# Gated delta rule: layout of the keys' norm row in DRAM, and a wait ahead of the next weights' load

## The reference, cut to what matters

```
mixed = silu(conv(x @ W_qkvz))            # causal convolution, four taps
q, k, v = ...                             # q, k: [B, S, 16, 128]
k = k * rsqrt(sum(k * k, axis=-1) + 1e-6) # one factor for each token and key head
# then, in chunks of tokens, with decay and beta:
M = -tril((k_beta @ k.T) * decay, -1);  T = inverse(I - M)
attn = (q @ k.T) * decay;  state update and output from k, q, v, T, attn
x = layernorm(x + gated_output @ W_out);  x = layernorm(x + ffn(x))
```

## Time and profile before

| | us |
|---|---|
| median of three runs | 4628.52 |
| lowest and highest of them | 4620.41, 4631.1 |
| the profiled execution, own time | 4659.61 |
| its span, first to last instruction | 4657.8 |
| PE busy in the span | 4215.2 |
| ACT busy | 3830.0 |
| DVE busy | 3657.7 |
| POOL busy | 2368.6 |
| mean granted TensorE clock | 0.979 of full speed |

### The profile page before, as it was taken

The page is one execution under the profiler, slowest core; times in us unless marked ns, Lnnn a source line. Parts: engine busy times, 40 slices in busy tenths (PEclk is TensorE's granted clock), DMA queues, the critical chain, the costliest instruction groups (busy, mean ns, idle before and its releaser), DMA issues. The chain is left out here.

```text
span 4657.8 us, 139558 instructions
## 1 busy us (share of the span) xinstructions
PE 4215.2 (90%) x44242; PEld 3757.0 (81%) x44242; DVE 3657.7 (79%) x6626; ACT 3830.0 (82%) x10831; POOL 2368.6 (51%) x3362
## 2 busy tenths in 40 slices
PE   3399999999999999999999999999999999999497
PEld 2288888888888888888888888888888888888476
DVE  4288888888888888888888888888888888888454
ACT  1388888888898888988889888898898988888244
POOL 4355555555545555455555555555555555555244
PEclk9699999999999999999999999999999999999799
DMA  6544443433434344343343443433434434343000
GB/s 196 187 138 125 130 140 122 138 125 130 143 122 134 125 129 144 121 134 128 127 144 124 131 133 123 143 123 132 134 123 142 125 130 139 121 140 107 32 14 23
DMA packets 365392, 584.77 MB, mean 126 GB/s; under 512 B 148240, under 2 KB 228624, under 8 KB 347920
## 3 DMA queue, kind: packets, MB, share of 16 engines
q1 hardware_dynamic: 364560, 583.70, 38.9%
q10 hardware_dynamic: 768, 0.26, 0.0%
HBM read 533.81 MB, written 50.07 MB: 125 GB/s over the span
## 5 line engine op out<-in xcount | busy, mean ns | idle before, releaser
L924 DVE SCALAR_TENSOR_TENSOR conv<-ps,cws,conv 128x511 f32<-128x511 f32 (+2 forms) x1536 | 1084.9, 741 | 68.2 <-ACT conv L812 56.8
L1116 POOL TENSOR_TENSOR xo<-xo,zs 128x512 f32<-128x512 f32 x256 | 326.3, 1275 | 1559.5 <-DVE xo L1018 1559.5
L630 PE MATMUL ps<-xb,wb 128*128 128x512 f32 x3072 | 841.1, 409 | 76.9 <-DMA wb<-w_scratch 73.3
L630 PEld LDWEIGHTS ps<-xb,wb 128*128 128x128 f32 x3072 | 541.8, 190 | 169.8 <-issue 73.5
L967 DVE CAST_PREDICATED pl<-masks,ps 128x512 f16<-128x512 uint16 x768 | 544.7, 709 | 56.2 <-PE ps L692 32.5
L873 ACT ACTIVATE t<-ps 128x512 f16<-128x512 f32 x768 | 465.3, 606 | 119.3 <-PE ps L700 108.5
L877 ACT ACTIVATE u<-ps 128x512 f16<-128x512 f32 x768 | 463.5, 604 | 43.7 <-PE ps L705 43.7
L790 PE MATMUL ps<-wo,xt 128*128 128x256 f32 x3072 | 427.9, 289 | 25.3 <-issue 23.4
L644 PE MATMUL ps<-wb,xb 128*128 128x256 f32 x3072 | 430.1, 290 | 0.0
L812 ACT ACTIVATE conv<-ps,cws 128x512 f32<-128x512 f32 x512 | 360.0, 703 | 69.7 <-PE ps L630 61.5
L790 PEld LDWEIGHTS ps<-wo,xt 128*128 128x128 f32 x3072 | 382.5, 189 | 39.4 <-issue 34.5
(11 more groups left out here) (158 smaller groups left out, 11557.9 us busy)
## 6 DMA issues: line engine op xcount, KB each, us to landing
xb<-x_scratch SPq DMA_DIRECT2D x128, 1024.0 KB, 5.9
wb<-w_scratch SPq DMA_DIRECT2D x128, 1024.0 KB, 7.5
grow<-rows_scratch SPq DMA_DIRECT2D x128, 512.0 KB, 3.7
wb<-w_scratch SPq DMA_DIRECT2D x128, 512.0 KB, 4.2
wo<-wout_scratch SPq DMA_DIRECT2D x128, 512.0 KB, 6.2
rk<-rk_scratch SPq DMA_DIRECT2D x128, 256.0 KB, 5.5
w_scratch<-wsplit SPq DMA_DIRECT2D x128, 192.0 KB, 3.4
wpiece<-in_Wqkvz SPq DMA_DIRECT2D x128, 96.0 KB, 2.1
```

The lines of the kernel that those rows point to most:

```text
L630: last = nc.tensor.matmul(proj_bank[c][:, :], wb[:, pw, k * WCOL + c * D:k * WCOL + (c + 1) * D], xb[p][:, px, k * S:(k + 1) * S], start=( ...
L924: nc.vector.scalar_tensor_tensor(out=conv[c][:, back:S], in0=proj_bank[c][:, 0:S - back], scalar=cws[p][:, c * TAPS + 3 - back:c * TAPS + ...
L1116: nc.gpsimd.tensor_tensor(x, x, zs[p][:, 2 * g:2 * g + 2, :, :], ALU.mult).then_inc(gated.sem, 1)
```

## The change

Three edits, in three places of `delta_rule`:

1. `load_w` of item a now also waits until the load of `rk` of item a - 1 has landed. That is the load that SP issued directly before it.
2. `store_norm` writes `rn` transposed: token i of chunk n goes to place n x 128 + i of the row in DRAM, where before it went to place i x 4 + n. The four numbers of a partition, which were one run of 16 bytes, are four runs of 4 bytes.
3. `keys` reads `rk` in steps of one element, where before it read every fourth element.

```
             def load_w(a, p, _):
                 proj_mm.wait(sp, a - 1, 4)
+                rk_in.wait(sp, a - 1, 16)
                 sp.dma_start(w_dst[:, :, 0:S], ...).then_inc(w_in.sem, 16)
...
             def store_norm(a, p, _):
                 sp.wait_ge(rnorm.sem, rnorm.at(a, 1))
                 rk_in.wait(sp, a - 1, 16)
-                sp.dma_start(rk_dram[0].rearrange("(i n) -> i n", n=NC), rn[:, :]).then_inc(rk_out.sem, 16)
+                sp.dma_start(rk_dram[0].rearrange("(n i) -> i n", n=NC), rn[:, :], allow_slow_non_contiguous=True).then_inc(rk_out.sem, 16)
...
                 nc.vector.tensor_tensor(kq[p][:, :, 0, :], conv[K][:, :].rearrange("p (n c) -> p n c", n=NC),
-                                        rk[:, :].rearrange("p (c n) -> p n c", n=NC), ALU.mult).then_inc(kq_ready.sem, 1)
+                                        rk[:, :].rearrange("p (n c) -> p n c", n=NC), ALU.mult).then_inc(kq_ready.sem, 1)
```

## The result

The changed kernel takes 5699.21 us (median of four runs, 5693.95 to 5701.22) against 4629.81 us before in the same session. The ratio is 1.2312, with a 95% interval of 1.2293 to 1.233: 23% slower, over a thousand microseconds, or 8.4 us for each of the 128 items. The forecast was 4579 us, faster by 1%, and even the slowest rival ended at 4832.

What follows compares the result with a forecast made beforehand. PE's idle time behind the chain store, row's load, `keys`, `gram` was taken as the bound; store +1.0, load -1.0, `keys` -0.39, weights 0 gave -49 us, 4610.5 against the profiled execution, 4579 us against the median; range 4480 to 4780.

Steps and rivals of the forecast that it cites:

- What bounds the kernel: In the loop, the chain store of `rn`, load of `rk`, `keys`, `gram` sets the step through PE's idle time, 1.3 us an item.
- Edit 3: At `keys` on the DVE, reading `rk` without the stride of four saves 0.39 us an item, all of it reaching PE.
- Edit 2, the store: At the store of `rn`, 512 packets of 4 bytes land in 2.4 us instead of 1.4, +1.0 us an item.
- Edit 1: At the load of `rk`, without the weights' load close behind, landing takes 4.5 us instead of 5.5, -1.0 us.
- The sum: Over the loop: store +1.0, load -1.0, `keys` -0.39, weights 0, so -0.39 us for each of 126 items, -49 us.
- its sign that PE stays busy 30.89 us in a step: In the loop's step, PE's busy time was to stay at 30.89 us after the change.
- The first rival: At store and load of the row, 512 small writes land or settle late: +1.6 us an item, 4832 us; chance 0.30.
- The second rival, late weights: At L630, weights land late and PE waits 1.3 us an item: +115 us in all, 4743 us; chance 0.07.
- The rival of the vanished wait: Ahead of `gram`, the round trip shrinks by 2 us and PE's 165.6 us wait goes: 4463 us; chance 0.15.

## Why the prediction was wrong, point by point

- **What bounds the kernel: right.** The chain of store, row's load, `keys` and `gram` sets the step, and PE's idle time there is the step's. Taken away, it gave 96 us; lengthened, it cost a thousand.
- **Edit 3: right.** 0.38 us and 47 us measured alone, against 0.39 and 49.
- **Edit 2, the store: this is the step that failed.** "I take 2.4, since at the time of this store SP has nothing else in flight: +1.0 us." It is 8.2 us, +6.8. The bound above was taken from two stores of 512 packets of 384 bytes. They match the number of packets and not their size: the term was sized by the count, and the runs show that 512 pieces of 4 bytes cost 1.9 us from issue to issue when they lie 64 bytes apart and 8.2 when they lie side by side. No row before the change has such a store, so its size could not have been read off; the 3.4 us of the slower of the two nearest rows was no upper bound.
- **Edit 1: right in direction, too small.** The load went from 5.5 to 3.9 with edit 1 alone, -1.6 where -1.0 was put for both effects. In the changed kernel it is 4.7, so the term of -1.0 came out as -0.8.
- **The sum.** Store +6.8, load -0.8, `keys` -0.38: +5.6 us of round trip for an item, against +5.8 us of idle time measured. PE's clock adds 2.4 us, and the two make 8.1 of the 8.4 us; the rest is the long profiled execution before. The prediction did not look at the clock: it named no wait so long that the clock would fall, and its sign that PE stays busy 30.89 us in a step failed (32.96 us in the mean of two steps).
- **The first rival: right in what happens, wrong in price.** It said that 512 small writes into one row of 2 KB land or settle late, and gave it 0.30. Its price of +1.6 us came from the same stores of 384 bytes. The rule of the Trainium skill quoted there ("DMA: Bandwidth & Descriptors", "Rules for kernel authors": a non-contiguous last dimension becomes one descriptor per element) holds, with 528 packets in the trace. But the descriptors are not what costs: 512 of them to places 64 bytes apart cost 0.5 us over the old store. The rule of the same page of the Trainium skill that spoke the other way ("Anatomy of one DMA — SWDGE (gpsimd) path": the write's receipt is most of a DMA's fixed time) describes another issuing path, but it names the right place: here it is the receipt that comes late, the last one 6.9 us after the last packet.
- **The second rival, late weights: wrong.** Their load takes 5.7 us (median) when it starts behind the row's landing, inside the 6.2 that the prediction gave it.
- **The rival of the vanished wait: priced too low.** With edit 1 alone the wait is gone (8.4 us left), but the kernel takes 4535.6 us and not 4463. The prediction took all of the 165.6 us off; that number comes from the long profiled execution, PE is busy 22.0 us longer, and in the run with pieces of 16 bytes 64 apart another wait comes up, 34.8 us of PE for ACT ahead of the projection.

## What to carry to other kernels

Before a store to DRAM is cut into pieces of 4 bytes, ask of the destination which pieces are neighbours: here it was not so much their number, and not their bytes, that cost. The same 512 values side by side cost 8 us on a path that is read back at once, and 64 bytes apart under 2. The nearest row of a profile is near only if it shares the property that costs, and 384-byte pieces did not share it. When a change does two things to one chain, time each alone: here a gain of 2% was hidden under a loss of 23%.

## What the runs showed of the hardware that I had not expected

- The packets of a store of 2 KB were through in 0.4 us, and the last report came 6.9 us later (median); in the step shown it was 9 us, with no packet of any transfer recorded in between.
- Stores of 128 pieces, side by side in both cases: 0.41 us from the last packet to the load's issue with pieces of 16 bytes, 6.82 with pieces of 4.
- A read of a row right after its landing can be slow: 5.5 us when the row was written as pieces of 16 bytes four to 64 bytes and another transfer follows, 3.3 to 3.5 when each piece had 64 bytes of its own and a quarter of what is read was fresh.
- After 7.8 us without work PE was granted 0.51 of its clock for the next 4.5 us; over the kernel PE's busy time grew by 303 us, more than a quarter of the loss.
- The DVE's two-input product of 128x512 f32 takes 1075 ns with one input in steps of 16 bytes and 692 with steps of 4.
